# A four-layer network on one core: bond items as one column sum on VectorE and four biased gelus, parted VectorE chains, and another table of step times

## The reference

```
strain = disp_win - disp[:, :, :, None, :]
bond_act = gelu(strain @ w_strain + b_strain + state[:, :, :, None, :] @ w_state_i
                + state_win @ w_state_j + rel_emb @ w_pos)
bond_logits = (bond_act @ w_bond_out)[..., 0] + b_bond_out[0]
damage_act = gelu(strain @ w_damage + b_damage)
damage = sigmoid((damage_act @ w_damage_out)[..., 0] + b_damage_out[0])
logits = bond_logits - damage * 10.0
weights = softmax(where(cmask, logits, -inf)); out = (weights over windows of val) @ w_cproj + b_cproj
```

## Time and profile before

| | |
|---|---|
| median of 3 runs | 3959.35 us (3958.97 to 3961.12) |
| the profiled execution's own time | 3941.28 us |
| its span | 3939.5 us |
| PE busy | 3131.8 us (79%) |
| DVE busy | 2503.1 us (64%) |
| ACT busy | 1661.7 us (42%) |
| POOL busy | 689.7 us (18%) |

### The profile page before, as it was taken

How to read it: one execution, slowest core, us unless ns; L and a number is a source line. 1 busy time by engine, 2 the same in 40 slices (tenths; PEclk the granted TensorE clock), 3 DMA queues, 4 the chain that set the end, 5 groups by cost and what they waited for, 6 DMA issues and landing times.

```text
span 3939.5 us, 43890 instructions
## 1 busy us (share of the span) xinstructions
PE 3131.8 (79%) x16174; PEld 1566.9 (40%) x16174; DVE 2503.1 (64%) x4568; ACT 1661.7 (42%) x2458; POOL 689.7 (18%) x465
## 2 busy tenths in 40 slices
PE   4458768987799778997699868997689867996588
PEld 1124323553245333553245432553235432454145
DVE  5534876578656876669755776568765786534542
ACT  3415515464344524464154534455154643431241
POOL 2001201311023101312013110322013110211030
PEclk8568879997799879998699978998799987997696
DMA  2330174302741164301842055501743027411261
GB/s 90 36 97 31 31 133 119 105 8 79 122 138 55 23 118 122 116 16 43 144 131 76 1 106 103 157 29 32 132 121 103 7 78 122 135 57 43 58 193 48
DMA packets 332142, 330.82 MB, mean 84 GB/s; under 512 B 101448, under 2 KB 267144, under 8 KB 331656
## 3 DMA queue, kind: packets, MB, share of 16 engines
q1 hardware_dynamic: 331928, 328.01, 34.8%
HBM read 278.88 MB, written 47.78 MB: 83 GB/s over the span
## 4 chain that ended last, share of the span: by engine, by line
PE 55%; DVE 23%; DMA 7%; ACT 5%; SPq 4%; issue 4%; POOL 2%; ACTq 0%; DVEq 0%; POOLq 0%
PE PS L1774 6%; PE PS L1797 6%; PE PS L1628 5%; PE PS L1801 5%; PE PS L1636 5%; DMA U<-band_scratch 4%; PE PS L1075 4%; PE PS L1742 3%; DVE MX L1568 3%; SPq L658 3%; PE PS L1753 3%; DVE U L885 2%; DVE XN L558 2%; DVE U L878 2%; DVE D L1619 2%
## 5 line engine op out<-in xcount | busy, mean ns | idle before, releaser
L1380 POOL TENSOR_TENSOR D<-D,GW 128x512 f32<-128x512 f32 x320 | 429.5, 1343 | 1419.1 <-ACT D L1453 1190.9
L770 ACT ACTIVATE U<-U 128x2048 f32<-128x2048 f32 x256 | 488.7, 1909 | 188.6 <-DVE U L878 104.4
L1614 DVE SCALAR_TENSOR_TENSOR D<-D,PS 128x512 f32<-128x512 f32 x336 | 228.9, 681 | 400.9 <-ACT D L1457 283.6
L1453 ACT ACTIVATE D<-PS 128x512 f32<-128x512 f32 x336 | 200.1, 595 | 615.9 <-PE PS L1797 615.9
L1774 PEld LDWEIGHTS PS<-WST,D 128*128 128x128 f32 (+1 forms) x2688 | 350.4, 197 | 163.9 <-DVE D L1619 99.7
L1774 PE MATMUL PS<-WST,D 128*128 128x128 f32 (+1 forms) x2688 | 378.5, 285 | 31.6 <-DVE D L1619 31.5
L1801 PE MATMUL PS<-XT,WST 128*128 128x512 f32 (+1 forms) x672 | 373.4, 638 | 28.8 <-DVE D L1614 27.8
L1075 PE MATMUL PS<-U,resident 128*32 128x512 f32 x2048 | 306.1, 678 | 112.1 <-ACT U L770 112.1
L885 DVE SCALAR_TENSOR_TENSOR U<-PP,RD,QB 128x512 f32<-128x512 f32 x512 | 361.7, 771 | 46.4 <-ACT QB L767 27.6
L1568 DVE TENSOR_REDUCE MX<-PS 128x2 f32<-128x1024 f32 x256 | 299.5, 1220 | 121.9 <-PE PS L1720 121.8
L1797 PE MATMUL PS<-XT,WST 128*128 128x512 f32 (+1 forms) x672 | 366.6, 628 | 9.8 <-DMA WST<-in_pairs_dram 6.5
(11 more groups left out here) (350 smaller groups left out, 4035.4 us busy)
## 6 DMA issues: line engine op xcount, KB each, us to landing
GW<-gates_scratch SPq DMA_DIRECT2D x320, 256.0 KB, 4.2
WST<-in_pairs_dram SPq DMA_DIRECT2D x336, 192.0 KB, 2.4
U<-band_scratch SPq DMA_DIRECT2D x32, 1280.0 KB, 14.9
UU<-in_w_dram SPq DMA_DIRECT2D x64, 512.0 KB, 7.4
UU<-q_scratch SPq DMA_DIRECT2D x24, 384.0 KB
UU<-k_scratch SPq DMA_DIRECT2D x24, 384.0 KB
e_scratch<-D SPq DMA_DIRECT2D x8, 1024.0 KB, 4.5
D<-e_scratch SPq DMA_DIRECT2D x32, 256.0 KB, 3.9
```

The source lines that it names most:

```text
L770: e.activation(ring(i), ring(i), ACT.Gelu).then_inc(S["act"], 1)
L1380: e.tensor_tensor(AV[:, n % 3, :], AV[:, n % 3, :], GW[:, p // 2 % GWS, p % 2, :], ALU.mult).then_inc(S["gated"], 1)
```

## The change

**Bond items.** The bond sum is one TENSOR_TENSOR of 2048 columns of PP and QB, as the damage sum always was (one line, L894, makes both now). The constant of the offset moves to ACT: instead of one gelu of 2048 columns, a bond item has four gelus of 512 columns, each with its column of RD as bias (L783). A damage item's gelu stays as it is (L779).

**Chains part.** DVE's chains get more yields, so that steps of the other part may stand between their instructions: `dve_kept`, `dve_gates`, `dve_update`, `dve_split`, the maxima, the mixing, layer 2's features. The first reciprocal is cut into two instructions of 512 columns. Nothing else in these chains is computed in another way.

**The table.** STARTS is new for every engine and TURN is 415.30 instead of 429.40. SP's and POOL's instructions keep their order. On PE, ACT and DVE, A's and B's steps interleave in another way.

```
-TURN = 429.40
+TURN = 415.30
...
     "a_dve": (
-        0.00, 2.97, 20.83, 27.43, 29.52, 31.86, 34.09, 37.57, 39.79, 42.02, 43.21, 47.02, 52.73, 74.28, 77.04, 77.68,
-        80.43, 82.77, 84.55, 87.29, 90.15, 93.80, 98.42, 103.35, 104.03, 106.97, 110.85, 117.43, 120.78, 123.52, 128.27, 128.96,
...
+        0.00, 3.80, 18.97, 25.56, 28.98, 29.54, 29.98, 30.54, 36.60, 37.04, 41.34, 46.12, 50.86, 72.41, 72.87, 73.51,
+        73.95, 77.49, 78.13, 82.41, 87.01, 91.93, 96.55, 101.47, 102.16, 105.11, 107.18, 107.95, 112.22, 112.66, 113.10, 114.90,
+        115.34, 115.96, 116.52, 117.59, 119.10, 123.84, 126.67, 128.54, 128.98, 129.42, 133.30, 138.65, 141.38, 145.26, 166.15, 167.10,
...
@@ -570,6 +573,7 @@
 
         def dve_kept(e, sco, m8, rpl, p, nt, ne, k):
             step(e, e.memset(m8[0:p, 0:nt, k:8], GONE))
+            yield
             for j in range(nt):
                 last = e.match_replace(rpl[0:p, j, 0:ne], m8[0:p, j, :], sco[0:p, j, 0:ne], GONE)
             step(e, last)
@@ -767,7 +774,14 @@
                         e.activation(QB[:, h, :], PS(2 + h), ACT.Copy).then_inc(S["l0_sb"], 1)
                 yield
                 e.wait_ge(S["pre"], at("pre", b, i + 1))
-                e.activation(ring(i), ring(i), ACT.Gelu).then_inc(S["act"], 1)
+                g, u, h, c, kind = item(i)
+                if kind == 0:
+                    e.activation(ring(i), ring(i), ACT.Gelu).then_inc(S["act"], 1)
+                else:
+                    for x in range(4):
+                        o = 16 * u + 4 * (3 - x) + c
+                        last = e.activation(ring(i)[:, T * x:T * x + T], ring(i)[:, T * x:T * x + T], ACT.Gelu, bias=RD[:, HOR - 1 - o:HOR - o])
+                    last.then_inc(S["act"], 1)
             yield
             e.wait_ge(S["logit_out"], at("logit_out", b, 8))
             e.activation(D[:, 4 * T:8 * T], D[:, 4 * T:8 * T], ACT.Tanh, bias=SC1[:, 0:1], scale=0.5).then_inc(S["soft_act"], 1)
@@ -872,19 +886,12 @@
                 g, u, h, c, kind = item(i)
                 if i >= RING:
                     e.wait_ge(S["act_used"], at("act_used", b, i - RING + 1))
-                if kind == 0:
-                    src = EP[:, h, :]
-                    win = bass.AP(src.tensor, src.offset + PAD - 16 * u - 12 - c, [list(src.ap[0]), [4, 4], [1, T]])
-                    last = e.tensor_tensor(ring(i).rearrange("p (q t) -> p q t", q=4), win, QE[:, h, :].unsqueeze(1).broadcast_to([P, 4, T]), ALU.add)
-                else:
-                    if i == 8:
-                        e.wait_ge(S["l0_sb"], at("l0_sb", b, 10))
-                    for x in range(4):
-                        o = 16 * u + 4 * (3 - x) + c
-
-                        last = e.scalar_tensor_tensor(out=ring(i)[:, T * x:T * x + T], in0=PP[:, h, PAD - o:PAD - o + T],
-                                                      scalar=RD[:, HOR - 1 - o:HOR - o], in1=QB[:, h, :], op0=ALU.add, op1=ALU.add)
-                last.then_inc(S["pre"], 1)
+                if i == 8:
+                    e.wait_ge(S["l0_sb"], at("l0_sb", b, 10))
+                src, own = ((EP, QE), (PP, QB))[kind]
+                src = src[:, h, :]
+                win = bass.AP(src.tensor, src.offset + PAD - 16 * u - 12 - c, [list(src.ap[0]), [4, 4], [1, T]])
+                e.tensor_tensor(ring(i).rearrange("p (q t) -> p q t", q=4), win, own[:, h, :].unsqueeze(1).broadcast_to([P, 4, T]), ALU.add).then_inc(S["pre"], 1)
                 while outs < 8 and i >= GROUP_END[OUT_ORDER[outs]] + 3 and i >= 8:
                     yield
                     if outs < 2:
...
             e.tensor_tensor(GB(b), tiles(PS(3)), XN(b), ALU.add).then_inc(S["a_f"], 1)
             yield
             e.wait_ge(S["den"], at("den", b, 1))
-            step(e, e.reciprocal(RCA[:, :, :], PSall[:, 2:4, :]))
+            for h in range(2):
+                last = e.reciprocal(RCA[:, h, :], PS(2 + h))
+                if h == 0:
+                    yield
+            step(e, last)
+            yield
             e.tensor_tensor(OS[:, :, :], OS[:, :, :], RCA[:, :, :], ALU.mult).then_inc(S["on"], 1)
             yield
             e.wait_ge(S["proj"], at("proj", b, 1))
             step(e, e.tensor_tensor(SB(b), tiles(PS(0)), over(cn("b_cproj")), ALU.add))
             yield
```

More of the change, by code:

```diff
@@ L940, in a_dve @@
             e.wait_ge(S["a_t"], at("a_t", b, 1))
-            dve_update(e, b, 0.5).then_inc(S["a_x"], 1)
+            (yield from dve_update(e, b, 0.5)).then_inc(S["a_x"], 1)
             e.wait_ge(S["a_x"], at("a_x", b, 1))
@@ L945, in a_dve @@
             e.wait_ge(S["qk"], at("qk", b, 2))
-            dve_split(e, FL[0:64, :, :], lambda k: SPL[0:64, :, k, :], "split")
+            yield from dve_split(e, FL[0:64, :, :], lambda k: SPL[0:64, :, k, :], "split")
             yield
@@ L951, in a_dve @@
             e.wait_ge(S["qk"], at("qk", b, 4))
-            dve_split(e, FG[0:64, :, 0:P], lambda k: SPLG[0:64, :, k, :], "split")
+            yield from dve_split(e, FG[0:64, :, 0:P], lambda k: SPLG[0:64, :, k, :], "split")
             yield
@@ L1476, in b_dve @@
             e.wait_ge(S["b_t"], at("b_t", b, 1))
-            dve_update(e, b, 0.5).then_inc(S["b_x"], 1)
+            (yield from dve_update(e, b, 0.5)).then_inc(S["b_x"], 1)
             e.wait_ge(S["b_x"], at("b_x", b, 1))
@@ L1504, in b_dve @@
             last.then_inc(S["l2_dve"], 1)
-            dve_kept(e, SCO, M8, RPL, P, NT, E2, K2)
+            yield
+            yield from dve_kept(e, SCO, M8, RPL, P, NT, E2, K2)
             yield
@@ L1508, in b_dve @@
             e.wait_ge(S["gate_act"], at("gate_act", b, 1))
-            dve_gates(e, DIF, RPL, GT, SM, P, NT, E2).then_inc(S["gate_dve"], 1)
+            (yield from dve_gates(e, DIF, RPL, GT, SM, P, NT, E2)).then_inc(S["gate_dve"], 1)
             yield from b_dve_pairs(e, b, 2)
@@ L1514, in b_dve @@
             e.wait_ge(S["b_t"], at("b_t", b, 2))
-            dve_update(e, b, 1.0).then_inc(S["b_x"], 1)
+            (yield from dve_update(e, b, 1.0)).then_inc(S["b_x"], 1)
             e.wait_ge(S["b_x"], at("b_x", b, 2))
@@ L1519, in b_dve @@
             e.wait_ge(S["qk3"], at("qk3", b, 2))
-            dve_split(e, F3[:, :, :], lambda k: SPL3[:, :, k, :], "split3")
+            yield from dve_split(e, F3[:, :, :], lambda k: SPL3[:, :, k, :], "split3")
             yield
```

28 lines of the change are left out of this document (21 added, 7 removed), and 166 rows, old and new, of the table STARTS.

## The result

The changed kernel takes 3984.05 us (median of 5, 3977.75 to 3986.42) against 3959.35 us (median of 5, 3956.55 to 3965.92). The ratio is 1.0055, with a 95% interval of 1.0041 to 1.0070. It is 25 us slower, a small loss but clear of the scatter; 33 were forecast.

A forecast was written before the change was run, and what follows sets the result against it. PE, the fullest engine, bounds the layer 1 experts and the last stretch, DVE layer 2 and turn 0. Per full turn +3 and +2.7, seven turns +40, turn 0 -7: +33 on 3959.35, 3992 us; range 3930 to 4040.

The forecast's parts named there:

- The form: Bond items: sum pace 2.20 us instead of 2.65, four gelus 2.44 us an item; turn 0 gains 7 us.
- The turn's start: First item's matmuls beside layer 1's experts: standing later, they lose PE's 1.45 us wait for ACT.
- ACT's order beside the experts: Layer 1: relus behind up to eight gelus delay the last downs 3.2 us; net +1.7 at the update.
- DVE's order in layer 2: More items ahead: GT some 11 us later, first pair +9.3, pairs gain 6.9, their end +3 per turn.
- the items ahead of XN fall into the memset's time: Layer 2: 5.1 us of added work ahead of XN costs nothing, since POOL's memset holds XN anyway.
- From S1 to S2: Layer 3 on PE: projection ahead of S2 waits for the product behind the reciprocals; +2.7 us per turn.
- A late start of that last stretch is passed on to the turn's end: Layer 3, PE busy 176.35 of 188 us: a late start is not made up there.
- ACT becomes what PE waits for: Rival beside the experts: stalls of some 7 us per turn from biased gelus, +60, 4019 us; chance 0.14.
- Only its place: Rival: work only changes place, pairs give back the early items' cost, S2's wait covered; 3959 us; chance 0.10.
- Faster: Rival: 7.3 us per turn taken off what DVE bounds, 3901 us, or half of it, 3930; chance 0.20.

The follow-up runs named there:

- e6: Changed kernel with ScalarE's relus 23 to 32 ahead of the gelus, as in the kernel before; 3962.52 us.
- e8: Changed kernel with layer 0's output projection and the part A steps behind it among S2 late again, on PE and ACT; 3966.05 us.
- e10: Changed kernel with both repairs, relus 23 to 32 ahead of the gelus and S2's order as before; 3942.86 us.
- e1: Kernel before with only the new bond item (one sum of 2048 on DVE, four biased gelus on ACT), old orders and yields; 3922.99 us, ratio 0.9907.
- e12: Form alone with late memset (3873.98 us), plus TensorE's first item one pair of projections later and that pair's relu ahead of the first gelu; 3877.90 us.
- e11: Changed kernel with GpSimd's two memsets of UU behind XN of layer 2; 3957.76 us.
- e13: Changed kernel with relus first, S2's order as before and GpSimd's memsets behind XN; 3909.10 us.
- e7: Form alone (3922.99 us) with layer 0's output projection moved ahead of the first S2 matmul; 3965.26 us.
- e5: Form alone (3922.99 us) with ScalarE's relus 23 to 32 behind the biased gelus beside the experts; 3972.32 us.

## Why the prediction was right, step by step

The direction and its cause were right: the form is a gain, the order a larger loss. Turn 4 gives the size of each step, as offsets from QE in the two traces (the change minus before), and the experiments the price in time. Of the 61 us that the order costs with the new form, 21.5 go with the relus (e6), 18 with S2's order (e8), some 2 more with both together (e10), and 20 are left.

*The form.* Sum and gelus came as worked out (2.20 us of pace; 709 ns and 2.45 us for four). Turn 0 gave 4.1 us where 7 were forecast. What I had wrong is its worth: I let the form gain nothing but in turn 0 and layer 2, and booked its full-turn part together with the order's. Alone it is worth 35 us. In e1's trace the pairs of layer 2 end 2.65 us earlier in turn 4.

*The turn's start.* Forecast: the 1.45 us wait of the earlier trace rows goes. It failed. The pair of projections put in its place needs a relu that stands behind the first gelu on ACT, and PE waited 2.12 us. Step +0.7 us in place of -1.5. I had checked which wait went and not which relu the added pair needs. e12 shows that even the relu ahead brings nothing.

*ACT's order beside the experts.* Mechanism right, size low: the last relu +5.85 us for a forecast of +3.2, the last accumulation +4.35 for +1.7 net. Undoing it in the changed kernel gives 21.5 us; doing more of it to the form alone costs 49. Of the terms that a run prices by itself it is the largest.

*DVE's order in layer 2.* L1505 +11.5 us (forecast 7.1, with what came from above), GT +14.8 (11), the first pair +13.15 (9.3, where the forecast's own terms give 9.1). The pairs took 22.7 us instead of the 25.6 forecast, and ended +3.35 (forecast +3; +4.5 in the mean of six turns). So the late gates and the short pairs nearly cancel, as forecast, in larger amounts both. That the items ahead of XN fall into the memset's time was half right, and POOL's rows show which half. Before, then in the changed kernel:

```profile
1785.76 2.99 POOL L562 TENSOR_TENSOR RS<-VE,half 128x4 f32<-128x4 f32 x1 [81.82 <-DVE VE L554]
1788.71 3.51 POOL L1367 MEMSET UU<- 128x4096 f32 x1
...
1810.46 2.99 POOL L565 TENSOR_TENSOR RS<-VE,half 128x4 f32<-128x4 f32 x1 [87.92 <-DVE VE L557]
1813.41 3.51 POOL L1389 MEMSET UU<- 128x4096 f32 x1
```

The memsets don't start at the last downs, as I had it, but behind the root, which waits for the statistics on DVE. So they hide what stands between the statistics and XN, and they move with what stands ahead of the statistics: the later update and the one item more. Their end, and XN's with it, comes 6.1 us later in the turn, where I had counted 1.7 (the item at nothing). From there to L1505 it is 5.4 us more, as forecast. e11 and e13 put what the memset hid at 2 to 3 us a turn.

*From S1 to S2.* Mechanism right, size low. The wait is 7.33 us in front of L1162 and the first S2 matmul is +9.4 us where 5.7 were forecast (3 from above and 2.7). The product's end is 265.3 us after QE, 2.6 later than before and what was left of layer 2's delay; the rest is the projection. I had taken 0.98 us for it, where the earlier trace rows has 1.95 for the whole of it; at the low clock behind the wait it takes 3.52. And the 1.5 us that I took off as covered were not: S2's operands had come through DMA by 1977.4, so nothing but the projection held it. In time, the projection ahead costs 42 us in the form alone (e7); in the changed kernel the whole order of S2 is worth 18 (e8).

*"A late start of that last stretch is passed on to the turn's end"* was too strong for the changed kernel. S2 begins +9.4, its last exponential is +7.0, and the turn ends +3.4 in turn 4; in the mean of six turns it is +12.2, +10.1 and +6.9. The new table won some of it back behind S2's last exponential: from there to the turn's end every kernel with the old table takes 141.4 to 142.8 us in the mean of six turns, and every one with the new table 138.5 to 139.7. Which of its steps did that stays open.

The terms that I put too low were met by this give-back and by the form, which I put too low as well. That the sum came within 8 us of the measured one is in part luck. It is 8 too high by the medians; between the two traces, on which the terms were worked out, the loss is 44 us, and 33 is 11 too low.

The rivals. *ACT becomes what PE waits for* had the right place, but the waits came by the order of ACT's instructions and not by their length, which was as worked out. *Only its place* holds for layer 2 and not for the turn. *Faster* is what the form would have been without the table.

That putting the relus late costs 49 us in one kernel while putting them first gives 21.5 in the other is mostly a matter of how far each edit goes. In the mean of six turns e5's last accumulation is 6.7 us later than e1's, and the time grows by 7.0 a turn; e6's is 3.9 earlier than the changed kernel's, and the time falls by 3.1. What stays open is why the costs of e5 and e7 sum to more (91 us) than the whole loss of 61, which has layer 2's part in it besides. The 3 us a turn that the new table wins back behind S2 are a part of the answer at most.

## What to carry to other kernels

When one change brings a new form of an operation and a new order, build the square of the two before judging either: here a gain of 35 us lay under a loss of 60. In an in-order queue look at a step together with what follows from it: the projection put back alone cost 27 us, with its followers it gave 18. For each instruction put ahead, name what it waits for and what stands behind it (a relu, a projection), since a wait removed at one step reappears at the next that needs the same engine. And look at an instruction that takes several times its usual length before moving work around it: the 7.53 us of XN, seen in the first profile, was worth 49 us, more than any other repair here.
